# A fused graph layer and expert layer: row scatters in two turns of four, expert tiles fourteen turns behind, the last weights two a turn

## The reference

```python
def reference(x, adj, Wv, bv, aw, ab, Wk, bk, switch_w, switch_b, expert_w, expert_b):
    # x: 128 fields of 128 tokens by 256; adj: 128 x 128 per field
    X = layernorm(x)
    Xw = X @ Wv + bv
    e = leaky_relu((Xw @ aw[:d, 0])[:, None, :] + (Xw @ aw[d:, 0])[:, :, None] + ab[0], 0.2)
    alpha = adj * exp(e)
    transition = alpha / (alpha.sum(-1, keepdims=True) + 1e-12)
    H, Xk = 0, X
    for k in range(3):
        H = H + Xk @ Wk[k] + bk[k]
        Xk = transition @ Xk
    x = x + relu(H)
    xf = layernorm(x).reshape(16384, 256)
    probs = softmax(xf @ switch_w.T + switch_b)          # 16 experts
    routes, route_probs = probs.argmax(-1), probs.max(-1)
    pos = position of the token among those of its expert, in order
    keep = pos < 1228                                     # capacity of an expert
    y = expert_w[routes] @ xf + expert_b[routes]
    return x + where(keep, y, xf) * route_probs
```

## Time and profile before

| | |
|---|---|
| median of 3 runs | 777.93 us (775.52 to 778.54) |
| the profiled execution | 778.68 us, its span 776.9 us |
| mean granted TensorE clock | 0.982 of full speed |
| TensorE matmul busy | 723.0 us, 93% of the span |
| VectorE, ScalarE, GpSimd busy | 611.5, 479.7 and 429.6 us |
| DMA | 99.76 MB, 128 GB/s in the mean |

### The profile page before, as it was taken

How to read it: one execution, slowest core, us unless ns; L and a number is a source line. 1 busy time by engine, 2 the same in 40 slices (tenths; PEclk the granted TensorE clock), 3 DMA queues, 4 the chain that set the end, 5 groups by cost and what they waited for, 6 DMA issues and landing times.

```text
span 776.9 us, 18809 instructions
## 1 busy us (share of the span) xinstructions
PE 723.0 (93%) x4919; PEld 643.6 (83%) x4919; DVE 611.5 (79%) x2974; ACT 479.7 (62%) x1504; POOL 429.6 (55%) x524
## 2 busy tenths in 40 slices
PE   1999999999999999999999999999999999857883
PEld 1788888888999999999998999989989988746663
DVE  4688888888888888888888888888888887775562
ACT  1456777766666666666666666666666666653551
POOL 5224455556555566566556555665665564565553
PEclk9999999999999999999999999999999999977998
DMA  5723443534443344444434433444443322353430
GB/s 168 205 69 107 136 152 124 177 122 140 144 126 122 126 150 145 144 151 133 145 126 144 142 119 110 142 142 137 145 139 126 103 87 91 98 161 107 123 104 1
DMA packets 92926, 99.76 MB, mean 128 GB/s; under 512 B 10445, under 2 KB 85258, under 8 KB 92822
## 3 DMA queue, kind: packets, MB, share of 16 engines
q1 hardware_dynamic: 77752, 66.36, 28.5%
q0 software_dynamic: 13008, 30.07, 10.8%
q10 hardware_dynamic: 2064, 2.13, 1.0%
HBM read 49.53 MB, written 54.72 MB: 134 GB/s over the span
## 4 chain that ended last, share of the span: by engine, by line
PE 90%; DVE 2%; issue 2%; DMA 2%; SPq 1%; ACT 1%; POOL 1%; POOLq 0%; DVEq 0%; ACTq 0%
PE ps_z12a L1161 12%; PE ps_z12b L1161 11%; PE ps_z0a L1161 9%; PE ps_lgb L1161 9%; PE ps_z0b L1161 8%; PE ps_lga L1255 6%; PE ps_z0b L1262 4%; PE ps_z0a L1262 4%; PE ps_xt L1195 4%; PE ps_z12b L1221 4%; PE ps_xt L1189 4%; PE ps_z12a L1221 3%; PE ps_lgb L1295 3%; PE ps_t L1243 2%; PE ps_t L1212 2%
## 5 line engine op out<-in xcount | busy, mean ns | idle before, releaser
L529 POOL DMA_INDIRECT out<-lent,tok x143 | 145.2, 1016 | 178.2 <-DVE lent L1122 166.7
L512 POOL DMA_INDIRECT rowbuf<-rows,idx x128 | 129.6, 1013 | 55.1 <-issue 27.1
L577 ACT CAST xth<-ps_xt 128x256 fp32r<-128x256 f32 x128 | 47.7, 373 | 137.0 <-PE ps_xt L1195 136.9
L754 DVE TENSOR_TENSOR xtl<-ps_xt,xth 128x256 fp32r<-128x256 f32 x128 | 54.3, 424 | 61.1 <-ACT xft L580 59.7
L651 ACT ACTIVATE x<-rin 128x256 f32<-128x256 f32 x143 | 86.8, 608 | 2.8 <-DMA rin<-rowbuf 2.8
L1255 PEld LDWEIGHTS ps_lga<-swc,xft 128*128 128x128 f32 x512 | 76.5, 190 | 13.9 <-ACT xft L580 3.0
L480 POOL TENSOR_SCALAR x<-xin,nm,r 128x256 f32<-128x256 f32 x128 | 72.3, 565 | 27.2 <-PE ps_xt L1195 16.2
L593 ACT ACTIVATE od<-rows,oc,oa 128x256 f32<-128x256 f32 x128 | 77.0, 602 | 0.1
L476 POOL TENSOR_TENSOR r<-ve,mhalf 128x4 f32<-128x4 f32 x32 | 34.1, 1067 | 77.1 <-ACT ve L623 77.1
L1255 PE MATMUL ps_lga<-swc,xft 128*128 128x16 f32 x512 | 65.8, 242 | 2.6 <-ACT xft L580 2.6
L1195 PE MATMUL ps_xt<-ident,x 128*128 128x128 f32 x256 | 49.5, 276 | 9.2 <-POOL x L480 8.3
(11 more groups left out here) (211 smaller groups left out, 2403.9 us busy)
## 6 DMA issues: line engine op xcount, KB each, us to landing
rin<-rowbuf SPq DMA_DIRECT2D x143, 130.0 KB, 2.1
xin<-in_x SPq DMA_DIRECT2D x32, 512.0 KB, 3.9
out<-od SPq DMA_DIRECT2D x32, 512.0 KB, 4.3
ain<-in_adj SPq DMA_DIRECT2D x32, 256.0 KB, 4.3
ewr<-in_ewT SPq DMA_DIRECT2D x16, 256.0 KB, 2.7
out<-lent,tok POOLq DMA_INDIRECT x143, 2.7
rowbuf<-rin ACTq DMA_DIRECT2D x1, 2080.0 KB, 9.7
rowbuf<-rows,idx POOLq DMA_INDIRECT x128, 3.0
```

The costliest lines, as they stand in the source:

```text
L512: pool.indirect_dma_start(out=rowbuf, out_offset=bass.IndirectOffsetOnAxis(ap=idx[:, i:i + 1], axis=0), in_=rows[:, r, :], in_offset=None, ...
L529: pool.indirect_dma_start(out=out.rearrange("g n d -> (g n) d"), out_offset=bass.IndirectOffsetOnAxis(ap=tok[:, i % RY:i % RY + 1], axis=0 ...
L754: dve.tensor_tensor(xtl[:, g % 2, :], ps_xt[:, 0:D], xth[:, g % 2, :].bitcast(F32), ALU.subtract).then_inc(s_x0l, 1)
```

## The change

Three things are changed. `LAG_TILE` goes from 16 to 14, so tile i is multiplied in turn i + 30, `WOVEN` becomes 99, and 44 tiles follow. The four row scatters of a group, which went out one a turn in turns 10 to 13 behind the group's first field, go out two a turn in the first two of these turns. And the expert weight pieces, which were rounded one a turn, go two a turn from the 25th piece on, so that they are done in turn 28 on VectorE where it was turn 32.

```diff
-LAG_TILE = 16
+LAG_TILE = 14

-        def piece_at(it, k):
-            m = it * BODY + k - 1
-            return m if 0 <= m < E * KT else None
+        def pieces_at(it, k):
+            s = it * BODY + k - 1
+            first = s if s < 24 else 24 + 2 * (s - 24)
+            return [m for m in range(first, first + (1 if s < 24 else 2)) if 0 <= m < E * KT]

                 g = k - LAG_OUT
-                if valid(it, g):
+                if valid(it, g) and g % G == 0:
...
                     pool.wait_ge(s_tok, bat(it, g) + 1)
                     alone(pool)
+                if valid(it, g) and g % G < 2:
+                    for h in range(2):
+                        row_scatter(g - g % G + 2 * (g % G) + h)
...
+            def row_scatter(g):
+                r = g % BODY
+                i = g // G % 2 * G + g % G
+                pool.indirect_dma_start(
+                    out=rowbuf, out_offset=bass.IndirectOffsetOnAxis(ap=idx[:, i:i + 1], axis=0),
+                    in_=rows[:, r, :], in_offset=None, bounds_check=last_row, oob_is_err=False,
+                ).then_inc(d_scat[r // G], 16)

-                m = piece_at(it, k + 1)          # ScalarE
-                if m is not None:
+                for m in pieces_at(it, k + 1):
                     act.wait_ge(d_ew[m // KT % EPP], 16 * (m // KT // EPP + 1))
                     act.copy(piece(ewh_f, m), staged(m)).then_inc(s_ewh, 1)

-                m = piece_at(it, k)              # VectorE
-                if m is not None:
+                for m in pieces_at(it, k):
                     dve.wait_ge(s_ewh, m + 1)
```

More of the change, by code:

```diff
@@ L492, in slot_fn @@
                 g = k - LAG_OUT
-                if valid(it, g):
+                if valid(it, g) and g % G == 0:
                     r = g % BODY
-                    b2 = g // G % 2
-                    i = b2 * G + g % G
                     if it * BODY + g == 0:
@@ L499, in slot_fn @@
                         alone(pool)
[L500 to L509, removed]
-                        alone(pool)
[L512 to L515, removed]
+                    pool.wait_ge(s_slot, bat(it, g) + 1)
+                    if it * BODY + g > 0:
+                        pool.wait_ge(s_tok, bat(it, g))
+                        alone(pool)
+                        rp = (r - G) % BODY
+                        pool.tensor_scalar(rows[:, r:r + G, TOKEN], rows[:, rp:rp + G, TOKEN],
+                                           float(G * P), None, ALU.add).then_inc(s_tok, 1)
+                    pool.wait_ge(s_tok, bat(it, g) + 1)
+                    alone(pool)
+                if valid(it, g) and g % G < 2:
+                    for h in range(2):
+                        row_scatter(g - g % G + 2 * (g % G) + h)
                 if it * BODY + k > B:
```

## The result

| | before | after |
|---|---|---|
| median | 776.72 us (4 runs, 775.31 to 778.54) | 827.31 us (4 runs, 823.15 to 829.21) |
| ratio | | 1.0648 (95%: 1.061 to 1.0687) |
| profiled execution, its span | 778.68, 776.9 | 829.21, 827.5 |
| granted TensorE clock | 0.982 | 0.970 |

Ratios and intervals leave out single executions that stood far off, of 992.86 us for the kernel before, 2491.16 for lag_16 and 2958.12 for lag_15.

A forecast was written before the change was run, and what follows sets the result against it. TensorE was taken to bound the kernel; 778.7 + 2.1 (moved tiles) + 26.3 (late loads) + 0.5 (weights) + 3.8 (first group) + 0.5 (store-only groups) - 0.8 (transition) = 811.1, on the median's scale 810.3 us, range 780 to 826.

The forecast's parts named there:

- The order of SyncE: SyncE's queue: tile loads stay behind the store, following it by 1.5 us in place of 5.6.
- How late the load lands: Each group's first tile load: lands 4.6 to 5.0 us behind the store's issue, wanted at 2.1, so 2.5 to 2.9 late.
- store's landing + 0.3 us: Rule for when a group's first tile load lands, queued behind x, adj and store; stores averaged 4.7 us.
- order in one queue: SyncE's DMA queue: the tile load waits behind 1.28 MB of x, adj and store, consumed in ring order.
- What is absorbed: ScalarE's norm to TensorE's L1221: 1.53 us of lateness absorbed, the rest is TensorE's.
- What a late tile costs: Woven groups with an x load ahead: 1.25 us each, 21 x 1.25 = +26.3 us.
- 1 to 1.9 us a group: Range of the forecast's own mechanism, late tile loads in woven groups: 805 to 824 us, chance 0.68.
- The transition: Between woven stage and tail: VectorE's last table about 2.5 us later, bounds -2.8 and +6; with two tiles fewer, -0.8.
- The two new waits: Transition: ScalarE stands about 2.4 us at tile 100 in turn 129; tile 104 in turn 133 some 3.6 us late.
- +0.5 in all: Three groups with only a store ahead (tiles 88 to 99): late loads cost +0.5 us together.
- The moved tiles: Two tiles go from tail into turns 30 and 31: +2.1 us before turn 128, tail shorter by 3.3.
- the weights: Second weight piece in turns 24 to 28 on ScalarE and VectorE: +0.5 us, bounds 0 and 1.7.

The follow-up runs named there:

- lag_16: Changed kernel with LAG_TILE back at 16, paired scatters and weights two a turn kept: 777.44 us, ratio 1.0016; again beside other runs 776.96 us.
- lag_15: Changed kernel with LAG_TILE 15 instead of 14, a group's first tile read one turn later: 778.32 us, ratio 1.0023.
- loads_first: Changed kernel with SyncE's tile loads moved ahead of the x and adj load and the store, lag 14 kept: 777.26 us, ratio 1.001.
- weights_only: Kernel before the change with only the weight pieces two a turn from the 25th piece: 775.77 us, ratio 0.9992.
- loads_before_store: Changed kernel with the tile loads between the x and adj load and the store of the same turn: 787.59 us, ratio 1.0133.
- small_store_again: Changed kernel with stores of 8 partitions of 128, x and adj loads whole, run a second time: 795.77 us, ratio 1.0249.
- scatters_one_a_turn: Changed kernel with row scatters back at one a turn, lag 14 and weights two a turn kept: 928.83 us, ratio 1.1962.

## Why the prediction was right and wrong

**The order of SyncE (right).** "The loads come not two turns earlier but only until just behind the store": forecast 1.5 us behind it, measured 1.21. loads_first shows it from the other side: move the block, and all is back.

**How late the load lands (right in size, wrong in its reason).** Forecast 2.5 to 2.9 us late, measured a wait of 62.4 / 21 = 2.97. The stores' landing, 4.7 us in the mean of eight before, is 4.7 in the mean of 21 after, and "store's landing + 0.3 us" held: the read starts 0.3 to 0.7 us behind that landing in 20 of 21 groups, 1.9 in the one from 216.88. The waits are 2.3 to 2.8 us where the store took 4.2 to 4.6, 3.0 to 3.1 where it took 4.8 to 5.0, 3.6 to 4.0 where it took 5.5 to 5.9. But I read this as order in one queue, and that isn't enough: in a queue of its own the load took 4.7 us and more. The Trainium skill (DMA: Bandwidth & Descriptors, section Queues, rings and completion order) says that an engine goes round between the queues that have work, packet by packet. By that alone the lone load should have come through early; here it landed 0.7 us ahead of a store issued 0.4 us ahead of it. What holds in both runs is this: a load issued into 1.28 MB in flight lands about with the store, 0.3 to 0.7 us behind it in the same queue (one group apart) and up to 2 us ahead of it from its own. Whether the load's bytes come late, or only the news of its completion, is left open.

**What is absorbed (right, as far as it goes).** Forecast 1.53 us from the read to L1221, measured 1.55. Counted from ScalarE's idle time to the length of the group, which is what the run pays, only 1.35 are absorbed: 0.11 of the difference is how idle time is counted, 0.1 is the slow restart of TensorE, which the forecast left out.

**What a late tile costs (the step that failed).** The sum had "21 x 1.25 = +26.3 us", 2.78 us late less 1.53 and nothing else. Measured in the 20 groups 1.81 us each, 36.2 in place of 25.0. Of the 0.56 missing, 0.26 is that the tile was read 3.04 us late (by the forecast's own inputs, 4.7 + 0.3 - 2.1 = 2.9, the term should have been 1.37), 0.10 is the restart behind each stop, and 0.26, mostly, the falls of the clock in two groups; these make 0.62, and 0.05 comes back by the slack, 1.55 for 1.53, and by the 21.30 us of before, which I compare with 21.27 above. The sum had no term for the last two, and gave no reason for putting the clock at nothing. The forecast's range of "1 to 1.9 us a group" did hold the 1.81, but its 824 us, and 826 with it, were worked out with all else at its central value. All else was larger too: of the 18 us between 811.1 and 829.2, 11 are in the 20 groups and 7 in the edges.

**The edges (wrong in size).** Turns 113 to 125: +4.6, not 1.8, because the last group with an x load ahead had a wait of 3.8 us, and the clock fell (0.94 from 634.43 to 661.70). The transition: +6.1 from turn 125 on, not 2.5. The two new waits were foreseen at the right places: 2.79 us at the read of tile 100 (and 0.46 at tile 101's) for about 2.4 forecast, 2.17 at tile 104's for 3.6. From turn 129's store to turn 137's it is 23.36 us where it was 18.85, +4.5. The rest is the tile read in turn 125, at 710.17, the third of the groups with only a store ahead: it was in the "+0.5 in all", but ScalarE waits 2.94 us there and TensorE 1.15. The bound that I gave, +6, was met.

**The moved tiles, GpSimd, the weights (right).** From VectorE's last table on (693.81 and 748.49) the run is shorter by 4.1 us for 3.3 forecast. GpSimd's x0 makes TensorE wait only once, at the start, as before. The weights cost 0.7 to 1.3 us up to turn 29.

**No gain even in the best order.** loads_first, lag_16 and both together are at 777 to 778 us and the kernel before is at 776 to 777: none beats it. Why is not shown. The chain in the transition ends in the last table. With lag 16 and the scatter wait gone, this table follows the one two before it after 16.5 to 17.0 us, where it was 18.9 and, in weights_only, 18.6; so about 2 us are gained there. But the start of the last table, in lag_16, lag_16_again and loads_first (before: 693.81), differs by 1.7 us between two profiles of one and the same kernel, which is as much as there is to explain:

```profile
691.65 0.16 DVE L1084 SCALAR_TENSOR_TENSOR left<-pos,done 128x16 int32<-128x16 f32 x1
```

```profile
693.38 0.16 DVE L1084 SCALAR_TENSOR_TENSOR left<-pos,done 128x16 int32<-128x16 f32 x1
```

```profile
694.49 0.17 DVE L1084 SCALAR_TENSOR_TENSOR left<-pos,done 128x16 int32<-128x16 f32 x1
```

## What to carry to other kernels

Where one engine issues transfers in a written order, an earlier producer brings a load forward only to the next wait ahead of it in that order. Before the consumer is moved up, find that wait, and put the loads with the nearest use ahead of the bulk. Price a stop of TensorE by more than its idle time in the profile: here each cost 0.25 us more at its two ends, and one of 2.4 us another 3.3 us by the clock. Read groups singly before their mean: a mean of 1.7 us was here made of waits of 1.1 and 2.4. And look for the bend: a load that is late by less than the consumer's idle time costs next to nothing and one that is later costs its excess each time, so one turn of lag decided 49 us.

## What the runs showed of the hardware

- A 130 KB load that takes 2.0 to 2.1 us alone took 3.4 to 4.9 us behind 0.77 MB in the same queue, and 4.7 to 6.6 us with 1.28 MB in flight from another queue.
- About every third group's store takes 5.5 to 5.9 us instead of 4.2 to 5.0, in the kernel before too (5.9 at 230.22, 5.6 at 357.80, 5.7 at 485.59). In loads_before_store and small_store_again the tile load of every third group is the slow one (4.8 to 4.9 us for 3.5, 3.2 to 3.4 for 2.2). Why is not known.
- TensorE's products took 0.63 us instead of 0.40 (a pair) from about 1 us to 8 us behind a stop of 2.42 us, at a granted clock of 0.52; behind stops of up to 1.96 us and two of 2.26 and 2.28 us the clock stayed at 1.00, and behind stops of 3.5 us and more it fell each time in scatters_one_a_turn (0.88 or 0.94 over a group).
- The first pair of matmuls behind a stop took 0.70 us instead of 0.59; those behind it took what they always took.
- On one chip three kernels ran 14 to 21 us slower than elsewhere, and a fourth above its forecast, with ScalarE and VectorE standing where no semaphore holds them, while the kernel before was near its usual time (778.44).
